# Row statistics spread over the groups, and three halves of the context products on GpSimd

## What is computed

```
x = x + tanh(g_xattn) * attn(ctx, ctx, layernorm(x), ssm_kernel, D)
x = x + tanh(g_ffn) * ffn(layernorm(x), router, experts, shared expert)

attn:  kv[i,j,h,l] = k[h,i,l] * v[h,j,l]            # 16 heads of 8 channels, k = v = ctx
       y = causal convolution of kv with ssm_kernel[h] along l, plus D[h] * kv
       out[h,j,l] = sum over i of y[i,j,h,l] * q[h,i,l]
ffn:   32 experts, top 6 of the best 4 of 8 groups, plus a shared expert
```

## Time and profile before

| | us |
|---|---|
| median of 3 runs | 513.12 (513.07 to 515.66) |
| the profiled execution | 514.59 |
| its span | 512.8 |
| busy: TensorE, VectorE, GpSimd, ScalarE | 435.5, 303.5, 275.5, 201.7 |

### The profile page before, as it was taken

One profiled execution on the slowest core, in us unless ns is written; L12 is line 12 of the kernel. 1 busy time (PEld: TensorE's weight loads), 2 busy tenths in 40 slices (PEclk: granted clock), 3 DMA queues, 4 the chain that ended last, 5 costly groups with the idle time before them and its releaser, 6 DMA issues.

```text
span 512.8 us, 8791 instructions
## 1 busy us (share of the span) xinstructions
PE 435.5 (85%) x2162; PEld 330.4 (64%) x2162; DVE 303.5 (59%) x1162; ACT 201.7 (39%) x522; POOL 275.5 (54%) x226
## 2 busy tenths in 40 slices
PE   0936989999999687799999999999999999999600
PEld 0726768768767565477777777777777777777400
DVE  4999898998986665334444444444444444444156
ACT  4531734644642511134444444444444444444300
POOL 2000027748758737558766666666566666666700
PEclk9986999999999698789999999999999999999955
DMA  6999913323369876858767666667666666666599
GB/s 257 383 354 396 384 40 130 130 75 107 120 214 366 299 262 201 256 195 133 127 118 127 113 114 116 118 114 125 114 112 115 116 123 119 116 115 103 67 331 334
DMA packets 59462, 91.56 MB, mean 179 GB/s; under 512 B 6797, under 2 KB 50189, under 8 KB 59149
## 3 DMA queue, kind: packets, MB, share of 16 engines
q1 hardware_dynamic: 35759, 55.07, 31.9%
q0 software_dynamic: 20160, 29.11, 31.6%
q10 hardware_dynamic: 3486, 6.73, 3.9%
HBM read 47.87 MB, written 43.02 MB: 177 GB/s over the span
## 4 chain that ended last, share of the span: by engine, by line
PE 69%; DVE 16%; DMA 7%; ACT 4%; issue 3%; DVEq 0%; SPq 0%; POOL 0%; POOLq 0%; ACTq 0%
PE bank L1261 24%; PE bank L1280 18%; PE bank L1250 5%; PE bank L1271 4%; DVE arena L702 4%; PE bank L1123 4%; PE bank L1103 3%; PE bank L1144 3%; PE bank L1091 3%; DMA arena<-token_sums 2%; DMA token_sums<-shd_sb,dest 2%; DMA payload<-expert_lists 2%; PE bank L1092 1%; ACT payload L548 1%; DVE arena L659 1%
## 5 line engine op out<-in xcount | busy, mean ns | idle before, releaser
L430 POOL DMA_INDIRECT expert_lists<-payload,slots x96 | 103.5, 1078 | 116.2 <-DVE slots L809 77.8
L1261 PE MATMUL bank<-wgu,work 128*128 x432 | 148.1, 466 | 1.3 <-DVE work L1018 1.3
L1280 PE MATMUL bank<-wd,work 88*128 x432 | 111.9, 382 | 0.0
L1036 DVE TENSOR_TENSOR work<-work,bank 128x176 f32<-128x176 f32 x108 | 36.5, 338 | 121.8 <-ACT work L593 121.8
L1261 PEld LDWEIGHTS bank<-wgu,work 128*128 128x128 f32 x432 | 74.8, 193 | 25.4 <-issue 2.9
L593 ACT ACTIVATE work<-bank 128x176 f32<-128x176 f32 x108 | 34.2, 317 | 111.4 <-PE bank L1261 111.4
L1280 PEld LDWEIGHTS bank<-wd,work 88*128 88x128 f32 x432 | 73.9, 191 | 6.2 <-issue 0.2
L445 POOL DMA_INDIRECT token_sums<-shgu_sb,dest x35 | 54.5, 1558 | 29.8 <-ACT shgu_sb L608 25.5
L1018 DVE COPY work<-bank 128x256 f32<-128x256 f32 x108 | 45.8, 424 | 28.9 <-PE bank L1250 28.9
L445 POOL DMA_INDIRECT token_sums<-q_sb,dest x28 | 43.6, 1558 | 23.6 <-ACT q_sb L608 15.9
L702 DVE TENSOR_TENSOR arena<-arena,q_sb 128x448 f32<-128x448 f32 (+7 forms) x120 | 45.4, 456 | 1.7 <-ACT arena L496 1.6
(11 more groups left out here) (174 smaller groups left out, 569.5 us busy)
## 6 DMA issues: line engine op xcount, KB each, us to landing
payload<-expert_lists SPq DMA_DIRECT2D x108, 152.0 KB, 2.6
wgu<-w_gu SPq DMA_DIRECT2D x9, 704.0 KB
expert_lists<-blank SPq DMA_DIRECT2D x1, 5016.0 KB, 23.4
wgu<-w_gu SPq DMA_DIRECT2D x1, 4928.0 KB, 18.9
arena<-token_sums SPq DMA_DIRECT2D x9, 512.0 KB, 8.8
wd<-w_down SPq DMA_DIRECT2D x4, 704.0 KB
token_sums<-blank SPq DMA_DIRECT2D x1, 2304.0 KB, 26.6
token_sums<-blank SPq DMA_DIRECT2D x1, 2176.0 KB, 23.0
```

The lines of the kernel that those rows point to most:

```text
L430: nc.gpsimd.indirect_dma_start(lists, bass.IndirectOffsetOnAxis(ap=slots[:, g % 2, b, k:k + 1], axis=0), pay[g % 2][:, b, :], None).then_i ...
L1036: nc.vector.tensor_tensor(win(work, H_AT + t % 2 * M, [[1, M]]), win(work, SG_AT + t % 2 * M, [[1, M]]), bank[2 + t % 2][:, M:2 * M], ALU. ...
L1261: last = nc.tensor.matmul(bank[2 + t % 2][:, 0:2 * M], xT_half(t, k), wgu[:, bass.ds(e * WGU_E + k * 2 * M, 2 * M)], start=(k == 0), stop= ...
L1280: last = nc.tensor.matmul(bank[6 + t % 2][:, 0:L], hT_half(t, c), wd[:, bass.ds(e * WD_E + c * L, L)], start=(c == 0), stop=(c == 1))
```

## The change

Statistics: the prologue makes row statistics of batches 4 to 7 only. Those of batches 8 to 11 are made in group 0 and those of 12 to 15 in group 1, ahead of L822, and their factors together with those of the group's own second layernorm: one pass of Newton steps over 8 columns. ScalarE waits for one count more of `norm_others_done` in each group.

Products: of the halves (group, s), GpSimd makes (0,1), (1,0) and (1,1), with the same eight multiplications each; VectorE makes (0,0) and all of groups 2 and 3. GpSimd waits for the first context, for all of `rest_in`, and for the convolutions that read the buffer before; the code stands ahead of its wait for the blank stores. `products_ready` becomes one semaphore for each half.

```diff
@@ GpSimd
+            def products(g, s):
+
+                for d in range(DH):
+                    last = nc.gpsimd.tensor_tensor(pairs(s, d), context(g, s, 0, DH - d), context(g, s, d, DH - d),
+                                                   ALU.mult)
+                last.then_inc(products_ready[s], 1)
+
+            pool.wait_ge(ctx_in, 16)
+            products(0, 1)
+            pool.wait_ge(rest_in, REST_IN)
+            pool.wait_ge(conv_ready, HALF)
+            products(1, 0)
+            pool.wait_ge(conv_ready, NH)
+            products(1, 1)
+
             pool.wait_ge(blanks_stored, 48)
@@ ScalarE
-                        act.wait_ge(norm_others_done, 1)
+                        act.wait_ge(norm_others_done, g + 1)
@@ VectorE
-                def layernorms(row, n, r, done):
+                def statistics(row, n, at):
 
                     for b in range(n):
-                        last = nc.vector.bn_stats(stats[:, b, :], rows[:, bass.ds(row + b, 1), :].rearrange("p a l -> p (a l)"))
-                    link(last, hold=True)
+                        last = nc.vector.bn_stats(stats[:, at + b, :],
+                                                  rows[:, bass.ds(row + b, 1), :].rearrange("p a l -> p (a l)"))
+                    return last
+
+                def factors(n, parts):
+
                     for b in range(n):
                         last = nc.vector.bn_aggr(moments[:, b, :], stats[:, b, :])
                     link(last)
...
+                            link(nc.vector.scalar_tensor_tensor(y, z, 1.5, y, ALU.add, ALU.mult))
+                    for at, r, done in parts:
+                        last = nc.vector.scalar_tensor_tensor(r[:, 0, :], z[:, at:at + GB], 1.5, y[:, at:at + GB],
+                                                              ALU.add, ALU.mult)
+                    link(last)
+                    for at, r, done in parts:
+                        nc.vector.scalar_tensor_tensor(r[:, 1, :], moments[:, at:at + GB, 0], -1.0, r[:, 0, :],
+                                                       ALU.mult, ALU.mult).then_inc(done, 1)
...
                     for s in range(2):
+                        if (g + 1, s) not in BY_POOL:
+                            for d in range(DH):
...
                 if route:
+                    if g + 2 < NG:
+                        statistics((g + 2) * GB, GB, GB)
...
                     link(last, hold=True)
-                    layernorms(g * GB, GB, norm, norm_done)
+                    link(statistics(g * GB, GB, 0), hold=True)
+                    parts = [(0, norm, norm_done)]
+                    if g + 2 < NG:
+                        parts.append((GB, normal_x(g + 2), norm_others_done))
+                    factors(len(parts) * GB, parts)
...
-                    layernorms(GB, B - GB, norm_x[:, :, GB:B], norm_others_done)
+                    link(statistics(GB, GB, 0), hold=True)
+                    factors(GB, [(0, normal_x(1), norm_others_done)])
@@ TensorE
-                    pe.wait_ge(products_ready, (g + 1) * 2 + s + 1)
+                    pe.wait_ge(products_ready[s], g + 2)
```

More of the change, by code:

```diff
@@ L98 @@
 CHUNKS = list(zip(ENDS, ENDS[1:]))
+BY_POOL = ((0, 1), (1, 0), (1, 1))
 IN_RANGE = "the tile table is made on the chip with every value clamped to its range"
@@ L185, in build @@
         norm_x_done, norm_done, xn_ready, qT_ready, q_ready = sem("norm_x_done"), sem("norm_done"), sem("xn_ready"), sem("qT_ready"), sem("q_ready")
-        products_ready, conv_ready, conv_copied = sem("products_ready"), sem("conv_ready"), sem("conv_copied")
+        conv_ready, conv_copied = sem("conv_ready"), sem("conv_copied")
+        products_ready = [sem(f"products{s}_ready") for s in range(2)]
         pairs_summed, attn_ready = sem("pairs_summed"), sem("attn_ready")
@@ L671, in layernorms, with normal_x @@
                         link(nc.vector.scalar_tensor_tensor(z, z, -0.5, v, ALU.mult, ALU.mult))
-                        link(nc.vector.scalar_tensor_tensor(r[:, 0, :] if i == 2 else y, z, 1.5, y, ALU.add, ALU.mult))
-                    nc.vector.scalar_tensor_tensor(r[:, 1, :], moments[:, 0:n, 0], -1.0, r[:, 0, :],
-                                                   ALU.mult, ALU.mult).then_inc(done, 1)
+                        if i < 2:
+                            link(nc.vector.scalar_tensor_tensor(y, z, 1.5, y, ALU.add, ALU.mult))
[6 more added lines that the diff above has]
+                                                       ALU.mult, ALU.mult).then_inc(done, 1)
+                def normal_x(k):
+                    return norm_x[:, :, k * GB:(k + 1) * GB]
                 def products():
                     for s in range(2):
[L679 to L682, removed]
+                        if (g + 1, s) not in BY_POOL:
+                            for d in range(DH):
+                                last = nc.vector.tensor_tensor(pairs(s, d), context(g + 1, s, 0, DH - d),
+                                                               context(g + 1, s, d, DH - d), ALU.mult)
+                            last.then_inc(products_ready[s], 1)
                         if not route:
@@ L812, in group @@
                 if not route:
-                    layernorms(0, GB, norm_x[:, :, 0:GB], norm_x_done)
+                    link(statistics(0, GB, 0), hold=True)
+                    factors(GB, [(0, normal_x(0), norm_x_done)])
                     dve.wait_ge(ctx_in, 16)
```

## The result

The changed kernel takes 524.81 us (median of 4 runs, 524.64 to 524.94) against 513.1 before: a ratio of 1.0207, 95% interval 1.0182 to 1.0232. It is slower by 11.7 us. Its profiled execution took 524.9 us with a span of 523.0; between the two profiled executions the distance is 10.3 us, since that of before lay 1.5 above its median.

What follows compares the result with a forecast made beforehand. TensorE, busy 85% of 512.8 us, was taken to bound the kernel, with VectorE the chain in the prologue until 43.11. Terms +0.95, +6.5 and +1.0 gave +8.4 us on the median 513.12: 521.5 us, range 511.2 to 530.

Steps and rivals of the forecast that it cites:

- forecast case: GpSimd's products and VectorE share reads, half of GpSimd's time landing on VectorE: 515.7 to 525 us, chance 0.33.
- first rival: GpSimd and VectorE alternate, each instruction waiting for the other's; VectorE loses all of GpSimd's time: +18, 531 us; chance 0.24.
- The cap on the prologue's gain: Multiplications by q can't begin before the eighth convolution copy ends at 24.6 instead of 26.86: at most 2.26 us gained.
- The halves of group 1 gain nothing: Moving (1,0) and (1,1) frees 6.15 us of VectorE, but beside 6.16 us of attention transposes: no gain on the path.
- Price of a half on GpSimd: Eight product multiplications of one half on GpSimd, estimated from MEMSET rows: 6.5 us, bounds 3.12 and 13.
- How much of it falls on VectorE: Share of GpSimd's product time lost by VectorE in the prologue: half, 3.25 us a half, 6.5 for group 1's two.
- Prologue: Half (0,1) on GpSimd delays the eighth copy to 27.8; multiplications by q start there instead of 26.86: +0.95 us.
- Group 1: Added statistics, aggregations and small instructions take 1.9 us; 0.9 hidden by the wait for scores, +1.0 us on the chain.
- The sum: Whole kernel: +0.95 (prologue) + 6.5 (halves of group 1) + 1.0 (group 1) = +8.4 us, giving 521.5.

## Why the prediction was right, and where not

The time lies in the range, 3.3 us above the forecast, and the path was right: the sum's terms, their places and their signs came as written. The mechanism of the forecast case was not right. It was sharing, with half of GpSimd's time on VectorE, and no row gave that half. The prediction's own signs for its first rival, fifteen multiplications of 11 us or more and Newton steps stretched to about 1 us, are what came: 13.62 us, and 1.01 down to 0.33. That the number is near in spite of this is partly luck, by two errors that offset each other. With the measured 5.56 us a half and half of it on VectorE the same sum gives +7.1 (0.5 + 5.6 + 1.0), with 6.5 us and 73% it gives +13.0 (2.5 + 9.5 + 1.0), and with both measured +10.9.

- **The cap on the prologue's gain** held: with VectorE's load lifted, the multiplications start when the eighth copy ends, in every kernel without GpSimd's halves. Its place, 24.6, is not fixed; where the convolutions sped up earlier it was 23.5.
- **The halves of group 1 gain nothing** held: VectorE idles 2.39 and 2.19 us before the gated additions of group 0, and from the first attention to the second it is 40.26 us after and 40.19 before (93.21 - 52.95, 83.30 - 43.11).
- **Price of a half on GpSimd**: 6.5 estimated, 5.56 measured: 0.9 too high.
- **How much of it falls on VectorE** was the mis-sized term. I took half, as a middle between nothing and all: 3.2 us for (0,1) and 6.5 for the others. It is 4.07 of 5.56 (norm ready at 14.86 instead of 10.79) and 8.1 of 11.12 (7.98 in the multiplications, 0.1 in a sum): 73% both times. The two engines' recorded times still overlap in part. Alone the fifteen multiplications take 5.64 and the products 11.12, together 16.8, and side by side both were through in 14.2. So what doesn't fall on VectorE is most likely the part of each instruction that needs no turn, and the pauses between two of GpSimd's; no run separates the two. The mechanism is that of the first rival, waits for the other's instruction, with the price between it and the forecast.
- **Prologue**: +0.95 forecast, +1.75 measured (28.61 against 26.86), by the same term.
- **Group 1**: +1.0 forecast. From the start of its attention to the choice it is 20.44 us after and 19.63 before, +0.81, and the choice no longer waits for scores. To the next attention it is +1.2 (40.07 against 38.87). No experiment could test it, since ScalarE's standstill lay over it.
- **The sum**: 8.4 forecast; 9.84 + 0.07 + 1.2 + 0.28 (group 2) = 11.4 measured up to the last attention, of which the stretch up to the experts gives 1 us back. From forecast to result it is 3.3 us, and 2.4 of them are the mis-sized share (0.8 + 1.6).

The Trainium skill's page "SBUF — State Buffer", section "Who interferes with whom", holds in these runs in the cases tried: a VectorE instruction with two SBUF inputs waits for a reading GpSimd instruction (2.31 instead of 0.17 us), not for one that only writes (5.63 us), and one with a single SBUF input such as the statistics is free (1.41 us for four). It also lists `tensor_scalar` among the operations that can enter the two-port mode, which fits the 0.76 us of L685. Where it has the one that comes later blocked for the whole instruction, the traces show a little less, 73% of GpSimd's time and not all of it. By that rule alone, without the traces' doubts, the forecast would have been the first rival, 531: too high by 6, where mine is too low by 3.

## What to carry to other kernels

Work moved to an idle engine costs what it takes from the engine that was to be relieved: here 11.1 us of products on GpSimd took 8.1 us from VectorE, and the 6.15 us they freed lay beside a wait. Before moving elementwise work to GpSimd, look at what VectorE does in that very stretch: beside statistics, PSUM operands or idle time it was free; small dependent instructions waited for nearly a whole product each. And first ask what comes next when the load is lifted: in the prologue the statistics alone gave all the gain that the eighth copy left to be had. How much of that gain reaches the end of the kernel is not settled.

## What the runs showed of the hardware

- GpSimd's copies of 1024 elements, with one read, hold VectorE too (a Newton step of 12 elements took 1.00 us instead of 0.17), its MEMSETs of the same size don't (0.17 us).
- The holding goes both ways: sixteen products on GpSimd took 14.22 us beside VectorE's multiplications and 11.12 mostly beside its statistics and gated additions.
- A VectorE TENSOR_SCALAR of 8 elements with one SBUF operand took 0.76 us beside GpSimd's products and 0.17 without, while statistics and aggregations were untouched.
- GpSimd's product of 512 elements took 1.04 us and that of 64 elements 0.42, an eighth of the elements for 40% of the time, so short instructions are dear there.
- On the three other chips ScalarE stood still in all kernels ahead of a group's q copies, 8.7 to 17.3 us and then 3.6 to 7.8 us more. The trace mostly names a releaser outside this core or an unknown queue, and what it is stays open.
